# Constant rows, permuted weights and bias copies move from POOL and VectorE to ScalarE

## The chip, the core and the metric

The kernel runs on one core of a Trainium2 chip. The core has five engines that run side by side, each in the order of its own instruction list: TensorE (PE, matrix products into PSUM), VectorE (DVE), ScalarE (ACT), GpSimd (POOL), and SyncE (SP), whose queue issues the DMA transfers. They meet through semaphores. The metric is the device time in microseconds. Three runs of the kernel before gave 901.6, 899.2 and 897.36 us, median 899.2.

## The reference

32 sequences of 256 positions x 256 features go through two blocks, each conditioned on a vector of 512 per sequence. Cut to what is computed:

```python
# layer 0, 8 heads of 32: linear attention
xn = ln(x, ln_w, ln_b)
q = softmax(xn @ Wq + bq, over the 32 features of a head)
k = softmax(xn @ Wk + bk + (1 - mask) * -1e6, over the positions)
v = (xn @ Wv + bv) * mask
y = q @ (k.T @ v)                      # per head
scale, shift = split(silu(emb) @ W_emb + b_emb)
x = x + silu(ln(y) * (1 + scale) + shift) @ W_out + b_out
# layer 1, 16 heads of 16: full attention, other weights
att = softmax(q @ k.T + (1 - mask) * -1e6)   # 256 x 256 per head
y = att @ v
x = x + silu(ln(y) * (1 + scale) + shift) @ out_w + out_b
```

## The kernel before

The work is cut into pieces, each a small function of a sequence number `b` (some also of a part `u`): `s0` (statistics of x), `r0`, `z0` (normalise), `k0`, `q0`, `v0` (projections of layer 0), `km`, `ke` (maximum and exponential of k), `att`, `y0`, `th0`, `st0`, `o0`, `x1` (its output), then `z1`, `q1p`, `k1p`, `v1p`, `rows`, `max`, `cols`, `exp`, `pv`, `yt`, `ty`, `Y1`, `th1`, `o1`, `o` for layer 1. At the bottom of each engine's block stands a written-out list of calls, such as `nmz(); cst(); fill(); r0(0); r0(1); z0(0)`, and this list alone sets the engine's order. Many sequences are in flight at a time. The PSUM bank of each piece comes from the table `BANK`, and the piece that must have freed it from `FREED`.

Projections are products of fp16 parts: a weight is scaled, its high part is written by ScalarE (`high_part`, pieces `wh_q0` to `wh_v1`), its low part by VectorE (`low_part`, pieces `wl_...`, which wait for `wh_...`). Before that come the scales: `w_max` (`w0m`, `w1m`), transposes on TensorE (`tr_...`), `largest` (`mx_...`), a spread over partitions (`ar_...`), `w_scale` (`w0p`, `w1p`). The products of a normalisation bias with weights are rows (`row0` to `row3`, line 928), summed with the bias (`bias_sum`, `fr0` to `fr2`), spread over the partitions (`bb0` to `bb2`, line 935) and copied to SBUF (`bias_copy`, `bc0` to `bc2`). `p3` splits the bias of k in three, and SP carries it to `augs`. The two conditioning tables are `fm0` and `fm1` (line 971), made into factors by `film_rows` (`f0m`, `f1m`) and `film_scale`.

Three parts of the set-up matter here. `fill` (line 2020, on POOL) writes the constant 2^15 into 32 of each 64 partitions of `SQ` and `SK`, the fp16 operands of layer 1's attention; the transfers into them wait for it (`split_in`). `perm` (line 1523, on VectorE) copies the q and k weights of layer 1 with their columns in another order into `XB1`, for the product `col`. `bias_copy` (line 1357, on VectorE) is a copy of 128x256 out of PSUM. A piece of the set-up tells the others that it is done by the counter `C` of its engine, at the place that the table `SETUP` gives it; `ready` waits for that.

Of the kernel before, what the change touches and what calls it, by code (L numbers as in the profile page):

```python
# [17 lines left out]
H1 = 16  # L18

HALF = 64  # L20
# [18 lines left out]
    "gv1": "72527115761226524122121136246323",
    "gr0": "46620260422044626446044242024444",  # L40
    "gr1": "24044600264202262024620426246462",
    "gr2": "46400264226044666646462262644020",
    "gr3": "62604662246226666004464226020044",
    "gr4": "40446460420640004662042444066602",
    "gr5": "62624420620024602666002626044024",
    "gr6": "46444206026246624464626644660662",
    "gr7": "60202466666446202466404426046406",
    "gc0": "06262420644400260046262442044666",
    "gc1": "62602042460624226464644666606040",
# [11 lines left out]
    "gty1": "13103676330420003004000052224650",
    "gy1T": "17523022013501451212002510120455",
    "go1": "62131214011661340161313412022400",
    "gpm": "0",
    "grow3": "2",
    "gcnd": "5",
    "gcol": "6",
    "grow0": "0",
    "gbb0": "3",
    "grow1": "1",  # L70
    "gbb1": "4",
# [2032 lines left out]
```

## Time and profile before

| what | value |
|---|---|
| median of three runs | 899.2 us |
| the profiled execution | 900.0 us |
| its span, from first to last instruction | 898.2 us |
| TensorE busy / mean granted clock | 830.1 us (92%) / 0.969 |
| VectorE busy | 810.9 us (90%) |
| POOL busy | 749.4 us (83%) |
| ScalarE busy | 685.3 us (76%) |
| DMA, mean | 96 GB/s |

The span is that of one profiled execution; a busy share is a mean over stages with different limits, so the windows say more than this table. In a timeline row a merged row "x4" gives the time of four instructions together, and the bracket the idle time before it and what ended it. The granted clock is a share of TensorE's full 2.4 GHz; 0.50 is 1.2 GHz.

### The profile page before, as it was taken

How to read it: one execution, taken by the hardware profiler on the slowest of the kernel's cores; microseconds unless marked ns; L12 is line 12 of the kernel's file. 1: busy time of each engine (PE TensorE's matmuls, PEld its weight loads, DVE VectorE, ACT ScalarE, POOL GpSimd, SP SyncE). 2: the span in 40 equal slices, each digit the busy share in tenths (PEclk: the TensorE clock that was granted, in tenths of full speed). 3: DMA queues.
4: the chain of work that ended last, by engine and by line, in shares of the span. 5: the costliest groups of instructions: out<-in, count | busy, mean ns of one | idle time of the engine just before them, and what ended most of it. 6: DMA issues, size and time to landing. Idle time of an engine off the chain costs nothing.

```text
span 898.2 us, 25197 instructions
## 1 busy us (share of the span) xinstructions
PE 830.1 (92%) x8651; PEld 600.1 (67%) x8651; DVE 810.9 (90%) x1646; ACT 685.3 (76%) x1236; POOL 749.4 (83%) x1210
## 2 busy tenths in 40 slices
PE   4798789899999999999999999999999999999885
PEld 1686766567767767777767777766777776655442
DVE  6999998999999999999999999989999999887862
ACT  0135448598889788889889889887888888888695
POOL 9957799888889889998999899988999887876314
PEclk8598899999999999999999999999999999999998
DMA  7220334433345454352443443464433432334301
GB/s 228 57 42 23 88 73 108 115 96 96 91 87 112 102 111 121 82 119 78 112 112 96 118 111 79 100 111 113 113 86 97 106 89 72 106 81 124 103 30 36
DMA packets 149306, 85.84 MB, mean 96 GB/s; under 512 B 87478, under 2 KB 141852, under 8 KB 149180
## 3 DMA queue, kind: packets, MB, share of 16 engines
q1 hardware_dynamic: 149180, 84.23, 38.1%
q8 instruction: 71, 1.16, 0.5%
q14 instruction: 55, 0.45, 0.2%
HBM read 39.52 MB, written 25.79 MB: 73 GB/s over the span
## 4 chain that ended last, share of the span: by engine, by line
PE 44%; DVE 26%; POOL 15%; issue 10%; ACT 3%; DMA 1%; SPq 1%; POOLq 0%; DVEq 0%; ACTq 0%
PE banks L686 13%; DVE NM L1245 9%; PE banks L833 6%; PE banks L694 5%; PE banks L820 4%; PE banks L809 4%; PE banks L701 3%; DVE st L1146 3%; PE banks L716 2%; PE banks L843 2%; POOL Z L1900 2%; POOL ZHL L1907 2%; PE banks L763 2%; PE banks L752 2%; POOL YN L1891 2%
## 5 line engine op out<-in xcount | busy, mean ns | idle before, releaser
L1245 DVE TENSOR_REDUCE NM<-banks 128x4 f32<-128x1024 f32 x256 | 302.1, 1210 | 14.6 <-PE banks L809 13.9
L1737 ACT ACTIVATE wraw<-banks,uu 128x1024 f32<-128x1024 f32 x154 | 170.8, 1134 | 24.7 <-PE banks L820 23.1
L1737 ACT ACTIVATE PX<-banks,uu 128x1024 f32<-128x1024 f32 x102 | 112.7, 1136 | 14.4 <-PE banks L820 12.7
L1945 POOL TENSOR_TENSOR SH<-ST,SH 128x512 f16<-128x512 f32 x64 | 74.4, 1168 | 33.1 <-ACT SH L1705 33.0
L686 PE MATMUL banks<-wo,SH 128*128 128x256 f16 x768 | 96.2, 277 | 5.2 <-POOL SH L1945 5.1
L1887 POOL TENSOR_TENSOR rs<-ve,nhalf 128x2 f32<-128x2 f32 x128 | 91.9, 718 | 10.7
L809 PE MATMUL banks<-SK,SQ 51*128 51x256 f16 x1024 | 89.8, 272 | 10.4 <-DVE NM L1245 4.0
L820 PE MATMUL banks<-SQ,SK 53*128 53x256 f16 x1024 | 90.5, 273 | 6.2 <-DVE NM L1245 2.2
L686 PE MATMUL banks<-wv,ZT 128*128 128x256 f16 x768 | 94.3, 273 | 2.1 <-DVE NM L1245 1.7
L1907 POOL TENSOR_TENSOR ZHL<-Z,ZHL 128x256 f16<-128x256 f32 x128 | 85.4, 688 | 5.3
L833 PE MATMUL banks<-wraw,V 128*32 128x256 f32 x1232 | 87.1, 385 | 2.6 <-DVE V L1187 1.4
L1719 ACT ACTIVATE R<-banks,fcs,sqs 128x256 f32<-128x256 f32 x128 | 73.2, 572 | 19.2 <-PE banks L694 18.9
L686 PEld LDWEIGHTS banks<-wo,SH 128*128 128x128 f16 x768 | 73.2, 99 | 21.6 <-POOL SH L1945 7.1
L686 PEld LDWEIGHTS banks<-wv,ZT 128*128 128x128 f16 x768 | 72.8, 98 | 17.3 <-issue 9.2
L1973 POOL TENSOR_TENSOR AB<-R,AB 128x512 f16<-128x512 f32 x64 | 76.0, 1193 | 5.2 <-ACT AB L1719 5.1
L1900 POOL TENSOR_SCALAR Z<-X,nm,rs 128x256 f32<-128x256 f32 x128 | 75.7, 599 | 3.2 <-issue 0.2
L1692 ACT ACTIVATE TH<-banks,hB,hA 128x256 f32<-128x256 f32 x128 | 66.4, 581 | 15.3 <-PE banks L701 15.2
L1891 POOL TENSOR_SCALAR YN<-Y,nm,rs 128x256 f32<-128x256 f32 x128 | 71.8, 569 | 2.6
L809 PEld LDWEIGHTS banks<-SK,SQ 51*128 51x128 f16 x1024 | 37.8, 94 | 53.8 <-issue 27.5
L1719 ACT ACTIVATE AB<-banks,fcs,sqs 128x256 f16<-128x256 f32 x128 | 73.6, 575 | 0.0
L820 PEld LDWEIGHTS banks<-SQ,SK 53*128 53x128 f16 x1024 | 37.1, 94 | 47.6 <-issue 26.4
L1663 ACT ACTIVATE KE<-banks,km,un 128x256 f32<-128x256 f32 x64 | 36.3, 585 | 40.4 <-DVE km L1161 37.8
(181 smaller groups left out, 1987.2 us busy)
## 6 DMA issues: line engine op xcount, KB each, us to landing
scr<-AB SPq DMA_DIRECT2D x64, 256.0 KB, 2.7
X<-in_x_dram SPq DMA_DIRECT2D x32, 256.0 KB, 2.9
SQ<-scr SPq DMA_DIRECT2D x64, 128.0 KB, 2.7
SK<-scr SPq DMA_DIRECT2D x64, 128.0 KB, 2.9
out_dram<-wemb SPq DMA_DIRECT2D x32, 256.0 KB, 2.5
SQ<-scr SPq DMA_DIRECT2D x64, 64.0 KB, 2.7
SK<-scr SPq DMA_DIRECT2D x64, 64.0 KB, 2.9
wemb<-in_L_cond_W_emb_dram SPq DMA_DIRECT2D x1, 1024.0 KB, 7.5
```

The costliest lines, as they stand in the source:

```text
L686: m = PE.matmul(dst[:, t, :], zt[:, j, k, t * P:(t + 1) * P], w[:, i, k, :], start=(k, n) == (0, 0), stop=(k, n) == (1, 2))
L809: m = PE.matmul(banks[:, n + j % 2, (j // 2) * T:(j // 2) * T + T], SQ[p, r, h, c * P:(c + 1) * P], SK[p, r, h, :], start=True, stop=True)
L820: m = PE.matmul(banks[:, n + j % 2, (j // 2) * T:(j // 2) * T + T], SK[p, r, h, c * P:(c + 1) * P], SQ[p, r, h, :], start=True, stop=True)
L833: m = PE.matmul(banks[32 * j:32 * j + 32, n, 0:T], V1[:, r, c, 4 * g + j, :], px((8 * b + u) % 5)[:, at_px(j):at_px(j) + T], start=(c == 0 ...
L1245: V.tensor_reduce(NMe[:, c, :, 2 * g:2 * g + 2], banks[:, n:n + 2, :].rearrange("p a (h m) -> p a h m", m=T), AX.X, ALU.max, negate=True). ...
L1719: t = A.activation(dst, bank(home(f"g{c}1", b))[:, f, :], ACT.Identity, bias=fcs[:, i, f:f + 1], scale=sqs[:, i:i + 1])
L1737: A.activation(px(v % 5), banks[:, n:n + 2, :].rearrange("p a n -> p (a n)"), ACT.Exp, scale=uu[:, 0:1]).then_inc(S["exp"])
L1887: G.tensor_tensor(rs[:, b % 2, l, :], ve[:, l, :], nhalf[:, :], ALU.pow).then_inc(S[f"r{l}"])
L1891: i = G.tensor_scalar(dst[:, t, :], src[:, t, :], nm[:, b % 2, l, t:t + 1], rs[:, b % 2, l, t:t + 1], ALU.add, ALU.mult)
L1900: i = G.tensor_scalar(Z[:, t, :], src[:, t, :], nm[:, b % 2, 2 * l, t:t + 1], rs[:, b % 2, 2 * l, t:t + 1], ALU.add, ALU.mult)
L1907: i = G.tensor_tensor(h[:, 1, k], z[:, :, k, :], h[:, 0, k], ALU.subtract)
L1973: G.tensor_tensor(AB[:, i, :, 1], R1[:, i], AB[:, i, :, 0], ALU.subtract).then_inc(S["sp" + c])
```

## The change

`fill` leaves POOL and becomes four pieces of ScalarE, `fill_q0`, `fill_q1`, `fill_k0`, `fill_k1`, each one instruction of 32 partitions x 6144 elements that reads a column of ones with the scale 2^15. `perm` and `bias_copy` go from VectorE to ScalarE word for word, as activations of the kind Identity. The transfers into `SQ` wait for the two fills of `SQ`, those into `SK` for the two of `SK`. The memset of `NMw` (`nmz`) goes behind those of the constants. All lists of calls and the tables `BANK` and `FREED` are written anew for this.

```diff
 SETUP = {
     "DVE": (
-        "mb0 mc w0m csl mx_w0 fr0 fr1 perm w0p w1m csT p3 bc0 wl_q0 bc1 o1m o0m wl_k0 fr2 wl_v0 f0m bm mx_w1 "
...
+        "mb0 csl csT w1m fr2 fr1 w0m mx_w1 fr0 mc mx_w0 w1p w0p o1m wl_q1 p3 wl_v0 wl_k0 o0m f1m f0m wl_q0 "
...
     "ACT": (
-        "th wh_k0 wh_v0 wh_q0 wh_o0 wh_k1 wh_q1 wh_v1 wh_o1 ").split(),
+        "th fill_k1 fill_q0 fill_k0 wh_q1 wh_k1 wh_q0 bc0 wh_v0 wh_k0 perm wh_v1 bc1 fill_q1 wh_o0 bc2 wh_o1 ").split(),
     "POOL": (
-        "nmz cst fill v1z ").split(),
+        "cst v1z nmz ").split(),
...
-        spare = sb("spare", [P, 2])
...
-                    ready(e, "fill")
+                    ready(e, f"fill_{c}0", f"fill_{c}1")
...
 @block.vector
-            def bias_copy(i):
-                ready(e, f"bb{i}")
-                V.tensor_copy(bbc[:, i, :], at_all(i)).then_inc(C["DVE"])
...
-            def perm():
-                e.wait_ge(l_row, 96)
-                e.wait_ge(l_w[1], 80)
-                for i in range(2):
-                    V.tensor_copy(prow[:, i, :].rearrange("p (e f h) -> p e f h", e=2, f=16),
-                                  brow1[:, i, :].rearrange("p (h e f) -> p e f h", e=2, f=16))
-                    for k, e0 in ((0, 0), (0, 1), (1, 0), (1, 1)):
-                        t = V.tensor_copy(XB1[:, i, k, e0 * P:(e0 + 1) * P].rearrange("p (f h) -> p f h", f=16),
-                                          wraw[:, 3 + i, k, :].rearrange("p (h e f) -> p e f h", e=2, f=16)[:, e0])
-                t.then_inc(C["DVE"])
...
 @block.scalar
+            def perm():
+                e.wait_ge(l_row, 96)
+                e.wait_ge(l_w[1], 80)
+                for i in range(2):
+                    A.activation(prow[:, i, :].rearrange("p (e f h) -> p e f h", e=2, f=16),
+                                 brow1[:, i, :].rearrange("p (h e f) -> p e f h", e=2, f=16), ACT.Identity)
+                    for k, e0 in ((0, 0), (0, 1), (1, 0), (1, 1)):
+                        t = A.activation(XB1[:, i, k, e0 * P:(e0 + 1) * P].rearrange("p (f h) -> p f h", f=16),
+                                         wraw[:, 3 + i, k, :].rearrange("p (h e f) -> p e f h", e=2, f=16)[:, e0], ACT.Identity)
+                t.then_inc(C["ACT"])
+
+            def bias_copy(i):
+                ready(e, f"bb{i}")
+                A.activation(bbc[:, i, :], at_all(i), ACT.Identity).then_inc(C["ACT"])
...
+            def fill(M, h):
+
+                ready(e, "cst")
+                r = slice(HALF * h + 32, HALF * h + 64)
+                A.activation(M[r].rearrange("p r h t -> p (r h t)"), one1[r, :].to_broadcast([32, 3 * H1 // 2 * T]), ACT.Identity,
+                             scale=2.0 ** 15).then_inc(C["ACT"])
+
+            def fill_q0():
+                fill(SQ, 0)
+
...
 @block.gpsimd
-            def fill():
-
-                follow(G.memset(spare[:, :], 0.0))
-                for M in (SQ, SK):
-                    for h in range(2):
-                        i = G.memset(M[HALF * h + 32:HALF * h + 64, :, :, :], 2.0 ** 15)
-                        if M is SQ or h == 0:
-                            follow(i)
-                i.then_inc(C["POOL"])
-                ready(e, "fill")
...
```

On ScalarE, the start of the program was (`th` writes SQ, then the high parts of the weights, then the first exponential):

```order
L1772 ACTIVATE SQ<-SQ 32x512
L1762 ACTIVATE wk<-wraw,sl 128x256 x2
L1762 ACTIVATE wv<-wraw,sl 128x256 x2
L1762 ACTIVATE wq<-wraw,sl 128x256 x2
L1663 ACTIVATE KE,ks<-banks,km,un 128x256 x2
L1672 ACTIVATE KT<-banks,mcol 128x256 x2
L1663 ACTIVATE KE,ks<-banks,km,un 128x256 x2
L1679 ACTIVATE QE<-QS 128x512
```

Now ScalarE begins with

```order
L1792 ACTIVATE SQ<-SQ 32x512
L1775 ACTIVATE SK<-one 32x6144
L1775 ACTIVATE SQ<-one 32x6144
L1775 ACTIVATE SK<-one 32x6144
L1739 ACTIVATE wq<-wraw,sl 128x128 x4
L1739 ACTIVATE wk<-wraw,sl 128x128 x4
L1739 ACTIVATE wq<-wraw,sl 128x256 x2
```

and behind the pieces of `perm` and one more weight its list reads, up to the first exponential,

```order
L1754 ACTIVATE XB<-wraw 128x128 x4
L1739 ACTIVATE wv<-wraw,sl 128x256 x2
L1760 ACTIVATE bbc<-banks 128x256
L1775 ACTIVATE SQ<-one 32x6144
L1640 ACTIVATE KE,ks<-banks,km,un 128x256 x2
L1649 ACTIVATE KT<-banks,mcol 128x256 x2
```

Three fills stand ahead of the first weight, and the high parts of both layers, bias copies, `perm` and the fourth fill all ahead of the first `KE`.

On POOL, behind the constants, the first normalisation (`nm`, `ve`, `rs`, then `Z`) was

```order
L2015 MEMSET augm 6x768
L2022 MEMSET spare 128x2
L2025 MEMSET SQ 32x6144 x2
L2025 MEMSET SK 32x6144 x2
L1885 TENSOR_SCALAR nm<-mv 128x2
L1886 TENSOR_SCALAR ve<-mv 128x2
L1887 TENSOR_TENSOR rs<-ve,nhalf 128x2
```

Now POOL goes, from the last constant to the memset of V,

```order
L2036 MEMSET augm 6x768
L1906 TENSOR_SCALAR nm<-mv 128x2
L1907 TENSOR_SCALAR ve<-mv 128x2
L1908 TENSOR_TENSOR rs<-ve,nhalf 128x2
L1906 TENSOR_SCALAR nm<-mv 128x2
L1907 TENSOR_SCALAR ve<-mv 128x2
L1908 TENSOR_TENSOR rs<-ve,nhalf 128x2
L1921 TENSOR_SCALAR Z<-X,nm,rs 128x256 x2
L1925 TENSOR_SCALAR ZHL<-Z 128x256 x2
L1928 TENSOR_TENSOR ZHL<-Z,ZHL 128x256 x2
L2042 MEMSET V 128x3072
L2043 MEMSET V 128x96
```

The memsets of `SQ` and `SK` are gone; that of `V`, which stood behind five normalisations, comes right behind the first.

On TensorE, ahead of the first large products (`wq` or `wk` with `ZT`), where line 971 (973 now) is a conditioning table and line 988 the product `col`, stood

```order
L989 MATMUL banks<-one,SQ 128x1
L988 MATMUL banks<-lnc,XB 128x1 x2
L989 MATMUL banks<-one,SQ 128x1
L988 MATMUL banks<-lnc,XB 128x1 x2
L989 MATMUL banks<-one,SQ 128x1
L971 MATMUL banks<-csT,wemb 128x32 x16
L863 MATMUL banks<-ident,mxw 3x128
L686 MATMUL banks<-wq,ZT 128x256 x12
L716 MATMUL banks<-ZT,wk 128x256 x6
L718 MATMUL banks<-augm,augs 128x256
L716 MATMUL banks<-ZT,wk 128x256 x6
```

Now TensorE has, between the last spread maxima and the first projections,

```order
L871 MATMUL banks<-mxd,ones 128x3
L937 MATMUL banks<-SQ,ones 128x256
L871 MATMUL banks<-mxd,ones 128x3
L973 MATMUL banks<-csT,wemb 128x32 x32
L718 MATMUL banks<-ZT,wk 128x256 x6
L720 MATMUL banks<-augm,augs 128x256
L718 MATMUL banks<-ZT,wk 128x256 x6
L720 MATMUL banks<-augm,augs 128x256
L688 MATMUL banks<-wv,ZT 128x256 x12
L865 MATMUL banks<-ident,mxw 1x128
L990 MATMUL banks<-lnc,XB 128x1 x2
L991 MATMUL banks<-one,SQ 128x1
```

Both conditioning tables are made ahead of the first projection, `col` is behind it, and k0 comes before q0.

On SP, the loads of layer 1's weights (`ld_w1`) now go out ahead of those of layer 0, with the load of the third sequence between them, and the six bias rows (`ld_r`) behind both.

## Rows read from the trace of the kernel before

**Rows 1.** The page, section 1: busy us, share of the span, instructions.
```profile
PE 830.1 (92%) x8651; PEld 600.1 (67%) x8651; DVE 810.9 (90%) x1646; ACT 685.3 (76%) x1236; POOL 749.4 (83%) x1210
```
**Rows 2.** Windows of the span: length, busy us by engine, granted clock, DMA.
```profile
0.00:41.20 41.20, 22.70 (x87) 17.04 (x88) 33.84 (x69) 4.41 (x8) 38.33 (x46) 0.70 0.53 145
32.00:39.00 7.00, 6.92 (x32) 6.90 (x32) 6.76 (x18) 0.23 (x1) 6.49 (x12) 0.50 0.21 39
41.20:160.00 118.80, 104.07 (x848) 84.95 (x848) 109.24 (x302) 63.28 (x139) 97.96 (x161) 0.89 0.31 72
160.00:800.00 640.00, 625.22 (x6830) 455.99 (x6832) 603.72 (x1165) 541.71 (x972) 567.14 (x934) 1.00 0.41 100
```
**Rows 3.** Timeline of POOL: start, duration, engine, line, operation, out<-in, idle before.
```profile
5.81 10.48 POOL L2025 MEMSET SQ<- 32x6144 f16 x2
16.35 11.97 POOL L2025 MEMSET SK<- 32x6144 f16 x2
28.41 0.19 POOL L1885 TENSOR_SCALAR nm<-mv 128x2 f32<-128x2 f32 x1
...
69.18 2.67 POOL L2032 MEMSET V<- 128x3072 f32 x1
```
**Rows 4.** Timeline of VectorE, the start and three later points.
```profile
14.57 1.75 DVE L1287 TENSOR_SCALAR mxd<-ident,mxc 3x3 f32<-3x3 f32 x1
...
17.07 5.39 DVE L1527 COPY SQ<-SK 1x256 f32<-1x256 f32 x1
22.39 0.77 DVE L1530 COPY XB<-wraw 128x128 f32<-128x128 f32 x4
...
23.26 5.09 DVE L1309 TENSOR_SCALAR pw<-sw 128x3 int32<-128x3 int32 x1
...
58.64 0.30 DVE L1309 TENSOR_SCALAR pw<-sw 128x3 int32<-128x3 int32 x1
...
79.33 0.75 DVE L1225 SCALAR_TENSOR_TENSOR X<-banks,un,XB 128x512 f32<-128x512 f32 x1
...
122.40 4.61 DVE L1245 TENSOR_REDUCE NM<-banks 128x4 f32<-128x1024 f32 x4
```
**Rows 5.** The page, section 5: ScalarE's largest group, count, busy, mean ns.
```profile
L1737 ACT ACTIVATE wraw<-banks,uu 128x1024 f32<-128x1024 f32 x154 | 170.8, 1134 | 24.7 <-PE banks L820 23.1
```
**Rows 6.** Timeline of ScalarE, three short pieces.
```profile
48.23 0.56 ACT L1663 ACTIVATE KE<-banks,km,un 128x256 f32<-128x256 f32 x1 [16.00 <-DVE km L1161]
...
54.86 0.62 ACT L1679 ACTIVATE QE<-QS 128x512 f32<-128x512 f32 x1
...
60.54 1.76 ACT L1762 ACTIVATE wk<-wraw,sl 128x128 f16<-128x128 f32 x4 [0.95 <-DVE iu L1330]
```
**Rows 7.** Timeline of SP's queue: two issues among the first loads.
```profile
7.74 0.47 SPq L495 DMA_DIRECT2D lnc<-in_L_cond_norm_b_dram  x1
...
16.32 1.53 SPq L499 DMA_DIRECT2D wemb<-in_L_cond_emb_w_dram  x1
```
**Rows 8.** DMA issues of the first 60 us: KB each, us to landing.
```profile
wemb<-in_L_cond_emb_w_dram SPq DMA_DIRECT2D x1, 1024.0 KB, 7.8
...
lnc<-in_L_cond_norm_b_dram SPq DMA_DIRECT2D x1, 1.0 KB, 4.4
```
**Rows 9.** Timeline of TensorE in the first 100 us.
```profile
9.71 4.31 PE L928 MATMUL banks<-wraw,lnc 128*1 128x256 f32 x12 [3.39 <-DMA lnc<-in_L_cond_ln_b_dram]
...
32.08 7.04 PE L971 MATMUL banks<-csT,wemb 128*128 128x32 f32 x32 [2.99 <-DVE csT L1490]
...
63.15 3.66 PE L971 MATMUL banks<-csT,wemb 128*128 128x32 f32 x32
...
90.76 1.12 PE L701 MATMUL banks<-ident,QE 128*128 128x128 f32 x4 [3.89 <-ACT QE L1679]
...
94.95 1.47 PE L694 MATMUL banks<-ZT,wq 128*128 128x256 f16 x12
```

More of the change, by code:

```diff
@@ L39 @@
[L39 to L49, printed above, removed]
@@ L61 @@
[L61 to L71, printed above, removed]
+    "gk0": "00614615174301150224341111057220",
+    "gkt": "67450610124020220001013203004504",
+    "gq0": "47140221473664301312012232346031",
+    "gqt": "14667341121140174315313330371050",
+    "gv0": "33116143505014241003200420210402",
@@ L88 @@
+    "ga_f0": "1",
+    "gt_f1": "7",
+    "ga_f1": "3",
+    "gt_b": "3",
+    "ga_b": "4",
     "gfm0": "1",
@@ L255 @@
     "PE": (
-        "pm row1 row0 row3 tr_w0 row2 ar_w0 bb0 bb1 cnd col fm0 tr_w1 tr_b tr_o0 tr_f0 ar_o0 ar_w1 ar_f0 "
-        "tr_o1 ar_o1 fm1 ar_b tr_f1 ar_f1 bb2 ").split(),
+        "cnd pm row2 row1 tr_w1 row0 row3 bb2 tr_w0 bb1 ar_w1 bb0 ar_w0 fm1 fm0 tr_o0 col tr_f0 ar_o0 ar_f0 "
+        "tr_o1 tr_f1 ar_o1 tr_b ar_b ar_f1 ").split(),
     "DVE": (
-        "mb0 mc w0m csl mx_w0 fr0 fr1 perm w0p w1m csT p3 bc0 wl_q0 bc1 o1m o0m wl_k0 fr2 wl_v0 f0m bm mx_w1 "
-        "mx_f0 mx_o0 o0p mx_o1 w1p film0 mx_b wl_k1 f1m wl_o0 mx_f1 fcs o1p wl_q1 mb1 wl_v1 bc2 film1 wl_o1 ").split(),
+        "mb0 csl csT w1m fr2 fr1 w0m mx_w1 fr0 mc mx_w0 w1p w0p o1m wl_q1 p3 wl_v0 wl_k0 o0m f1m f0m wl_q0 "
+        "wl_k1 mx_o0 wl_v1 mx_f0 o0p film0 mx_o1 wl_o0 bm mx_b o1p mx_f1 fcs mb1 film1 wl_o1 ").split(),
     "ACT": (
-        "th wh_k0 wh_v0 wh_q0 wh_o0 wh_k1 wh_q1 wh_v1 wh_o1 ").split(),
+        "th fill_k1 fill_q0 fill_k0 wh_q1 wh_k1 wh_q0 bc0 wh_v0 wh_k0 perm wh_v1 bc1 fill_q1 wh_o0 bc2 wh_o1 ").split(),
     "POOL": (
-        "nmz cst fill v1z ").split(),
+        "cst v1z nmz ").split(),
 }
@@ L1473, in fr2 @@
                 bias_sum(2)
-            def bc0():
-                bias_copy(0)
-            def bc1():
-                bias_copy(1)
-            def bc2():
-                bias_copy(2)
             def csl_():
@@ L1562, in fcs_ @@
                 V.tensor_scalar(tm[:, :], tm[:, :], 2.0 ** -15, None, ALU.mult).then_inc(C["DVE"])
-            mb0(); s0(0); s0(1); mc(); w0m(); csl_(); mx_w0(); fr0(); fr1(); perm(); w0p(); w1m(); csT_(); p3_()
-            bc0(); wl_q0(); s0(2); bc1(); o1m(); o0m(); wl_k0(); fr2(); wl_v0(); f0m(); bm(); q1(0); km(0)
-            mx_w1(); qm(0); v(0); s0(3); mx_f0(); s0(4); rk(0); mx_o0(); km(1); at_(0); v(1); q1(1); o0p(); rq(0)
-            qm(1); mx_o1(); w1p(); Y0(0); q1(2); rk(1); film0(); mx_b(); qm(2); s1(0); v(2); at_(1); km(2); rq(1)
@@ L1653, in _ @@
-            o_(31)
+            mb0(); csl_(); s0(0); s0(1); csT_(); s0(2); w1m(); fr2(); fr1(); w0m(); mx_w1(); fr0(); mc(); mx_w0()
+            w1p(); w0p(); o1m(); wl_q1(); p3_(); wl_v0(); wl_k0(); o0m(); f1m(); s0(3); f0m(); wl_q0(); s0(4)
+            wl_k1(); mx_o0(); km(0); wl_v1(); v(0); mx_f0(); rk(0); q1(0); o0p(); qm(0); v(1); film0(); q1(1)
+            mx_o1(); km(1); qm(1); at_(0); rq(0); km(2); q1(2); Y0(0); qm(2); s1(0); rk(1); rq(1); at_(1); wl_o0()
+            q1(3); Y0(1); v(2); qm(3); s1(1); st0(0); rq(2); rk(2); q1(4); at_(2); qm(4); bm(); km(3); x1(0)
@@ L1768, in high_out, with bc0, bc1, bc2 @@
                 A.activation(W["o", l][:, 0], worw[:, l], ACT.Identity, scale=sw[:, 6 + l:7 + l]).then_inc(C["ACT"])
+            def perm():
[11 more added lines that the diff above has]
+                A.activation(bbc[:, i, :], at_all(i), ACT.Identity).then_inc(C["ACT"])
+            def bc0():
+                bias_copy(0)
+            def bc1():
+                bias_copy(1)
+            def bc2():
+                bias_copy(2)
+            def fill(M, h):
[5 more added lines that the diff above has]
+                fill(SQ, 0)
+            def fill_q1():
+                fill(SQ, 1)
+            def fill_k0():
+                fill(SK, 0)
+            def fill_k1():
+                fill(SK, 1)
             def th():
@@ L1796, in wh_o1 @@
                 high_out(1)
-            th(); wh_k0(); wh_v0(); wh_q0(); ke(0); kt(0); ke(1); qe(0); qt(0); wh_o0(); kt(1); qe(1); wh_k1()
-            qt(1); qe(2); th0(0); ke(2); sh0(0); kt(2); ke(3); wh_q1(); wh_v1(); qt(2); kt(3); ke(4); th0(1)
-            sh0(1); qe(3); qa(0); qt(3); ka(0); qe(4); kt(4); th0(2); qt(4); ke(5); sh0(2); kt(5); qe(5); wh_o1()
-            qt(5); th0(3); sh0(3); qa(1); ka(1); ke(6); kt(6); qa(2); qe(6); th0(4); ka(2); sh0(4); qt(6); ke(7)
-            th0(5); kt(7); exp(0, 0); exp(0, 1); exp(0, 2); exp(0, 3); exp(0, 4); exp(0, 5); sh0(5); qe(7)
@@ L1868, in _ @@
-            yt(31, 1); yt(31, 2); yt(31, 3); sh1(29); th1(30); sh1(30); th1(31); sh1(31)
+            th(); fill_k1(); fill_q0(); fill_k0(); wh_q1(); wh_k1(); wh_q0(); bc0(); wh_v0(); wh_k0(); perm()
+            wh_v1(); bc1(); fill_q1(); ke(0); kt(0); qe(0); wh_o0(); qt(0); ke(1); bc2(); qe(1); qt(1); kt(1)
+            qe(2); ke(2); th0(0); kt(2); sh0(0); qe(3); qt(2); ke(3); th0(1); ke(4); sh0(1); qe(4); qt(3); kt(3)
+            kt(4); qa(0); th0(2); sh0(2); ka(0); ke(5); qa(1); ka(1); wh_o1(); kt(5); qt(4); qe(5); th0(3); sh0(3)
```

832 lines of the change are left out of this document (423 added, 409 removed), and 215 rows, old and new, of the table FREED.

## The prediction

> **What bounds the kernel now.** I read the page first. TensorE is busy for 92% of the span and VectorE for 90% [rows 1], so either could be the bound, and only stretches tell. In the windows of the span [rows 2] the reader is to see three kernels in one. From 160 to 800 us TensorE is busy for 625.2 of 640 us at full clock: it sets the pace there, and nothing off it matters. In the first 41.2 us it is busy for 22.7 us only, at a mean clock of 0.70, and between 41.2 and 160 it idles for 118.8 - 104.07 = 14.7 us and runs at a mean clock of 0.89. The change touches instructions of the start alone, so its worth is how much earlier TensorE is fed. A start that comes earlier passes through the full stretch one for one.
>
> Next I read POOL's timeline [rows 3]. Four memsets (helper `fill`, 32 rows x 6144 fp16 each, in two merged rows) take it from 5.81 to 28.32 us, and only then does it normalise the first sequence (28.41). Then VectorE's timeline in the same stretch [rows 4]. Instructions of a few elements last as long as a memset does: the cast of 3 columns at 23.26 takes 5.09 us and ends at 28.35, with POOL's memsets; the same form takes 0.30 us at 58.64. The copy of one row of 256 at 17.07 takes 5.39 us and ends at 22.46, again with a memset. The product with `ident` at 14.57 takes 1.75 us and ends at 16.32. Four copies of 128x128 at 22.39 are not held (0.77 together). So VectorE loses about 1.5 + 5.1 + 4.8 = 11.4 us behind fills. The trace shows this; it is the mechanism on which the forecast rests.
>
> The Trainium skill, "SBUF — State Buffer" (the section on engine ports), says that VectorE and GpSimd share one port pair as an exclusive lock, that the loser waits for the whole instruction, and that ScalarE never waits on anyone. By that rule the stall vanishes wholly when ScalarE writes the same bytes, and it stays for whatever POOL memset is left. The trace agrees for the copies and casts named, while the 128x128 copies show that not every VectorE instruction pays.
>
> **The change part by part.** (1) Removed from POOL: `fill`, 22.5 us. POOL is then free at about 5.3 us; it gets `z0(0)` to `z0(4)` done long before the weights need them. Alone this is worth nothing: after 28.41 [rows 3] z0(0) still came before its weights. What is late next is the weights' path.
>
> (2) Removed from VectorE: the waits of 11.4 us; `perm`, which without waits is 2 x 0.77 for the eight copies and about 2 x 0.2 for the rows, 1.9 us; three copies of a bias, 3 x 0.4 = 1.2 us. Together 14.5 us. Left on POOL is the memset of `V1`, 2.67 us [rows 3], now right behind `z0(0)`, at about 12 us. There VectorE is in a long reduction or waits for DMA, so I charge 0 and keep 2.7 us as the upper bound.
>
> (3) Added on ScalarE: four fills of 6144 elements a row. No such long instruction is in the trace. From 512 elements (0.62 us [rows 6]) to 1024 (1.134 us [rows 5]) an element costs 1.0 ns, so a fill is 0.62 + 5632 x 0.001 = 6.2 us. Bounds: the same slope from zero, 6.1 us; and the price per element of the 128-wide pieces of `wk`, 1.76 us for 4 x 128, 3.4 ns [rows 6], 21 us, which is far. I take 6.2, since a fill is one long instruction, nearest to the 1024 row. Three fills stand before the weights: from the end of `cst` (5.5 us) to 24.1. Then wh_q1 1.7, wh_k1 1.7, wh_q0 0.8, bc0 0.4, wh_v0 0.8, wh_k0 0.8: 30.3 us. Then `perm`, ten pieces of 0.35 to 0.45, 3.6; wh_v1 0.8, bc1 0.4, the fourth fill: 41.3 us. Queued behind it is `ke(0)`, for which the whole first chain waits.
>
> (4) Moved on SP: the weights of layer 1 come first, those of layer 0 five weight issues and one X issue later. In before the first set of weights releases TensorE at 9.71 [rows 9]; the second set's last vector is issued at 7.74 and lands 4.4 us later [rows 7, 8]. So layer 1 is now there at 9.7 and layer 0 at 7.74 + 0.51 + 4.4 = 12.7. The six bias rows go out last at 10.9; with the same 4.4 us they are there at 15.3. The last tables of the second embedding land, as now, near 24 (the 1 MB issue at 16.32 takes 7.8 [rows 7, 8]).
>
> Walk of the start, in the new order, each step at the sum of its own rows in the timelines of before. TensorE: rows of layer 1 from 9.7, those of layer 0 from 12.7, at 0.36 to 0.47 us a matmul of which a row has four (12 took 4.31 [rows 9]); with the broadcasts, 1.0 each, and the transposes, ar_w1 ends at 21.4 and ar_w0 at 23. VectorE: biases from 15.3, w0m and the maxima until 20.3, w1p (1.9) 23.3, w0p 25, o1m 25.7, wl_q1 27.6, p3 (4.1 now) 31.7, wl_v0 and wl_k0 by 33.4. TensorE meanwhile makes both embedding tables. One took 7.04 us at half clock, 3.66 at full [rows 9]. In before the first ran for 7 us at 0.50 throughout [rows 2], so I charge both 7.04: 23 to 37.1 us. So `k0(0)`, the first large matmul, starts at 37.1, 4.1 us before q0(0) at 41.2, with the second table done (3.66 us at 63.15 no longer to do): TensorE is 4.1 + 3.7 = 7.8 us ahead there.
>
> VectorE goes on: o0m, f1m, s0(3) to 37.5, f0m 40, wl_q0, s0(4), wl_k1 43.9, mx_o0, `km(0)` 45.2, wl_v1, `v(0)` 46.8. In before km(0) releases ke(0) at 48.23 [rows 6], and v(0) ends at 49.9: 3 us ahead. But by then it has also done w1p, wl_q1, f1m, wl_k1, wl_v1, mx_o0 and s0(3), 1.9 + 1.9 + 2.6 + 1.9 + 0.9 + 0.4 + 1.0 = 10.6 us that before does later, and has left out q1, qm and bm, 1.8. It is thus 3 + 10.6 - 1.8 = 11.8 us ahead in work. `ke(0)` waits for km(0) at 45.2 and not for the fourth fill at 41.3: the fill is hidden by 3.9 us. Following the new order with these durations, `x1(0)` comes at about 72 to 73 against 79.33 [rows 4], `q1p(0)` near 84 against 94.95 [rows 9], and the first maximum of `rows(0)` at 111 to 113 against 122.40 [rows 4]. Being 10 us early there, TensorE must lose less in the ramp: in before its clock fell to half after waits such as the 3.89 us in front of 90.76 [rows 9], for ScalarE's QE, itself late by VectorE's rq.
>
> Sum against the profiled execution, 900.0 us (span 898.2 plus 1.8 around it): 7.8 us at the start, 2 to 4 more of the 14.7 idle us of the ramp, nothing in the full stretch, nothing in the tail: -10.5, thus 889.5. The median of the three runs is 0.8 lower, so 889. For the new order in the long stretch and the tail, which the trace of before cannot show, I allow 3 us either way.
>
> **The rivals.** (A) As above, 889, own range 885 to 893. (B) Given back: TensorE starts 4 us early, but the ramp keeps its waits since the transposes, copies and scratch transfers that feed layer 1 are as long as before; then only the start counts, 900 - 4 = 896 to 899. For it: POOL is busy for 97.96 of the ramp's 118.8 us [rows 2] and can bound it whatever VectorE does. Against it: part of that load is backlog of the fill. (C) More: all 14.5 us of VectorE arrive at the end, since it is busy for 109.2 of 118.8 us in the ramp [rows 2], or the tables run at full clock, which brings k0(0) to where its `augs` rows land, about 35, and runs the first matmuls at twice the speed, 2 + 3 us. That gives 900 - 14.5 = 885.5, or with both some 882. The Trainium skill, "TensorE: Matmul & The Clock Gate" (Part 1), says that a TensorE kept busy is given the full clock. By that rule the tables would be this faster case; the 7 us at 0.50 in the trace speak against it. (D) Slower: the price of a fill. If a 6144-element row on ScalarE costs like short pieces, with the 256-wide step of 0.45 us (1.76 ns an element) it is 10.8 us. Then the weights leave ScalarE at 44.1 instead of 30.3, and the fourth fill ends at 5.5 + 4 x 10.8 + 11.0 of the rest = 59.7, with ke(0) behind it, against 48.23 in before [rows 6]. That is 11.5 us late, less the 3.7 of the table: 908. It decides from about 8.8 us a fill, where ke(0) would be 3.7 us late. (E) It doesn't do what it says, VectorE being held by other POOL work that moves into the gap: as B.
>
> **How the numbers follow.** A 0.58, B with E 0.13, C 0.23, D 0.06. The range 881 to 897 leaves out D, the upper edge of B and the far end of C, under 2 in 10. What this kernel's measurement can tell from no change is 0.5%, 4.5 us. Below 894.7 lie A, C: 0.82. Within are most of B and a sliver of A: 0.12. Slower: D, 0.06.
>
> **What would show it.** Right: ScalarE's fills at 6 to 6.5 us each; no VectorE instruction of a few elements over 1 us before 40 us; first k0(0) matmul at 35 to 38; q1p(0) near 84; TensorE's busy time from 160 to 800 about as now. Wrong: fills over 8 us, ke(0) released by a fill, k0(0) after 41, or the ramp with as much idle as before although VectorE is ahead.

## The result, and the profile after

The changed kernel takes 878.1 us (median of 4 runs, 877.98 to 878.67); the kernel before took 898.4 beside it (897.36 to 901.6). The ratio is 0.9761, 95% interval 0.9730 to 0.9792: 2.4% faster. Forecast were 889 and a range of 881 to 897. The sign was right; the gain of 20.3 us by the medians (21.5 by the ratio) is twice the predicted 10, and the time lies outside the range. One of the eight runs of `new_fillback` below took 1599 us and is left out of its figures.

The profiled execution of after took 878.06 us, its span 876.2, so 22.0 less than the span of before. Section 1 of its page, against [rows 1]:

```profile
PE 827.4 (94%) x8651; PEld 603.3 (69%) x8651; DVE 792.1 (90%) x1633; ACT 708.0 (81%) x1253; POOL 725.7 (83%) x1205
```

TensorE does the same work in nearly the same busy time (830.1 and 827.4), so 19.3 of the 22.0 us are idle time of TensorE and 2.7 are busy time. POOL has 23.7 us less to do, VectorE 18.8 less, ScalarE 22.7 more. ScalarE's timeline shows the new fills, against none in [rows 6]:

```profile
5.27 5.32 ACT L1775 ACTIVATE SK<-one 32x6144 f16<-32x6144 f32 x1 [1.08 <-POOL augm L2036]
10.62 5.32 ACT L1775 ACTIVATE SQ<-one 32x6144 f16<-32x6144 f32 x1
15.85 5.30 ACT L1775 ACTIVATE SK<-one 32x6144 f16<-32x6144 f32 x1
22.34 1.72 ACT L1739 ACTIVATE wq<-wraw,sl 128x128 f16<-128x128 f32 x4 [1.19 <-DVE iu L1332]
...
32.99 5.32 ACT L1775 ACTIVATE SQ<-one 32x6144 f16<-32x6144 f32 x1
43.18 0.56 ACT L1640 ACTIVATE KE<-banks,km,un 128x256 f32<-128x256 f32 x1 [4.88 <-DVE km L1163]
```

A fill takes 5.32 us (6.2 predicted). The first weight waits 1.19 us for VectorE's scale and `ke(0)` 4.88 us for VectorE's maximum: neither waits for a fill. VectorE's timeline, against [rows 4]:

```profile
19.70 0.17 DVE L1311 TENSOR_SCALAR pw<-sw 128x3 int32<-128x3 int32 x1
19.90 0.64 DVE L1312 TENSOR_SCALAR pw<-pw 128x3 f32<-128x3 f32 x1
20.57 0.59 DVE L1314 TENSOR_SCALAR pw<-pw 128x2 f32<-128x2 f32 x1
...
26.08 1.12 DVE L1444 TENSOR_SCALAR augs<-augs,iu 6x256 bf16<-6x256 bf16 x1
27.12 1.36 DVE L1445 TENSOR_SCALAR SQ<-SQ,iu 1x256 f32<-1x256 f32 x1
```

The cast that took 5.09 us behind a memset takes 0.17. What is left of such waits is 0.4 to 1.1 us each, behind POOL's ordinary tensor operations:

```profile
19.84 1.29 POOL L1928 TENSOR_TENSOR ZHL<-Z,ZHL 128x256 f16<-128x256 f32 x2
25.85 2.50 POOL L1947 TENSOR_TENSOR XB<-X,bobc 128x512 f32<-128x512 f32 x2 [4.71 <-DMA bobc<-in_L_cond_b_out_dram]
```

TensorE's timeline of the start, against [rows 9]:

```profile
9.65 1.86 PE L930 MATMUL banks<-wraw,lnc 128*1 128x256 f32 x4 [1.79 <-DMA lnc<-in_L_cond_norm_b_dram]
13.00 1.87 PE L930 MATMUL banks<-wraw,lnc 128*1 128x256 f32 x4 [1.49 <-DMA lnc<-in_L_cond_ln_b_dram]
...
20.05 13.59 PE L973 MATMUL banks<-csT,wemb 128*128 128x32 f32 x64
33.49 1.44 PE L718 MATMUL banks<-ZT,wk 128*128 128x256 f16 x6
```

The weights come at 9.7 and 13.0 (9.7 and 12.7 predicted) and both tables take 13.6 us (14.1 predicted). But they start at 20.05, not at 23, and `k0(0)` at 33.5, not 37.1.

**Where the 22 us are.** I cut both spans at the same work: at the first large product, at the output of sequence 0 (`o(0)`), of sequence 14 and of 25, the points read off VectorE's timeline. Before:

```profile
41.20:206.30 165.10, 147.02 (x1307) 115.21 (x1308) 153.88 (x383) 97.17 (x201) 136.58 (x227) 0.92 0.34 81
...
206.30:553.00 346.70, 342.79 (x3755) 253.27 (x3754) 329.28 (x648) 298.04 (x537) 315.92 (x521) 1.00 0.43 103
553.00:812.40 259.40, 250.45 (x2744) 178.34 (x2740) 241.99 (x461) 219.23 (x389) 224.42 (x366) 1.00 0.39 97
812.40:898.20 85.80, 67.11 (x770) 36.20 (x768) 51.95 (x91) 66.45 (x104) 34.13 (x54) 0.97 0.24 68
```

After:

```profile
33.50:191.80 158.30, 144.38 (x1295) 112.00 (x1296) 143.23 (x357) 99.44 (x197) 133.15 (x224) 0.93 0.36 83
...
191.80:538.30 346.50, 340.81 (x3739) 253.85 (x3739) 329.37 (x644) 293.92 (x532) 314.68 (x519) 1.00 0.41 101
538.30:792.00 253.70, 250.11 (x2764) 181.42 (x2764) 240.56 (x467) 220.24 (x389) 223.98 (x367) 1.00 0.43 104
792.00:876.20 84.20, 68.63 (x768) 38.52 (x756) 52.14 (x91) 65.51 (x103) 35.22 (x55) 0.90 0.22 63
```

The first number behind each window is its length. The lengths differ by 6.8, 0.2, 5.7 and 1.6 us, and the start before them by 7.7: together 22.0. So 14.5 us are gained up to 192 us (`o(0)`); the next 347 us of work take the same time; then, long after all that the change replaced is done, another 7.3 come. In the third window TensorE idles for 8.95 us before (259.40 - 250.45) and 3.6 after. Which part comes from the placement of the work (who does it) and which from the new order and banks is what the experiments have to tell.

### The profile page after: what moved, and what is told of

It reads as the page before. It is cut to its first block, busy times and chain, and to the rows that moved or that the text cites. A ratio compares the mean times of both kernels' runs of the same rounds, so it can differ in the third digit from the quotient of the medians.

```text
span 876.2 us, 25220 instructions
## 1 busy us (share of the span) xinstructions
PE 827.4 (94%) x8651; PEld 603.3 (69%) x8651; DVE 792.1 (90%) x1633; ACT 708.0 (81%) x1253; POOL 725.7 (83%) x1205
## 4 chain that ended last, share of the span: by engine, by line
PE 39%; POOL 19%; DVE 14%; issue 11%; ACT 5%; DMA 0%; SPq 0%; POOLq 0%; DVEq 0%; ACTq 0%
PE banks L688 11%; PE banks L835 7%; DVE NM L1247 4%; PE banks L696 4%; PE banks L822 4%; PE banks L811 4%; POOL ZHL L1928 3%; PE banks L703 3%; POOL Z L1921 3%; DVE st L1148 2%; PE banks L845 2%; POOL YN L1912 2%; POOL SH L1966 2%; POOL ZHL L1925 2%; POOL AB L1994 2%
## 5 line engine op out<-in xcount | busy, mean ns | idle before, releaser
L1714 ACT ACTIVATE PX<-banks,uu 128x1024 f32<-128x1024 f32 x102 | 112.9, 1138 | 11.4 <-PE banks L822 9.9
L688 PE MATMUL banks<-wv,ZT 128*128 128x256 f16 x768 | 98.6, 280 | 0.9 <-DVE NM L1247 0.8
L1696 ACT ACTIVATE R<-banks,fcs,sqs 128x256 f32<-128x256 f32 x128 | 73.5, 574 | 26.7 <-PE banks L696 20.3
L1928 POOL TENSOR_TENSOR ZHL<-Z,ZHL 128x256 f16<-128x256 f32 x128 | 87.8, 706 | 5.3
L688 PEld LDWEIGHTS banks<-wv,ZT 128*128 128x128 f16 x768 | 74.8, 100 | 17.3 <-issue 7.5
L835 PE MATMUL banks<-wraw,V 128*32 128x256 f32 x1232 | 85.1, 385 | 1.6 <-ACT wraw L1714 0.6
L1669 ACT ACTIVATE TH<-banks,hB,hA 128x256 f32<-128x256 f32 x128 | 66.2, 580 | 15.7 <-PE banks L703 14.2
L1906 POOL TENSOR_SCALAR nm<-mv 128x2 f32<-128x2 f32 x128 | 29.0, 226 | 49.0 <-DVE mv L1151 48.2
```

Source lines behind the costliest of these rows:

```text
L688: m = PE.matmul(dst[:, t, :], zt[:, j, k, t * P:(t + 1) * P], w[:, i, k, :], start=(k, n) == (0, 0), stop=(k, n) == (1, 2))
L835: m = PE.matmul(banks[32 * j:32 * j + 32, n, 0:T], V1[:, r, c, 4 * g + j, :], px((8 * b + u) % 5)[:, at_px(j):at_px(j) + T], start=(c == 0 ...
L1696: t = A.activation(dst, bank(home(f"g{c}1", b))[:, f, :], ACT.Identity, bias=fcs[:, i, f:f + 1], scale=sqs[:, i:i + 1])
L1714: A.activation(px(v % 5), banks[:, n:n + 2, :].rearrange("p a n -> p (a n)"), ACT.Exp, scale=uu[:, 0:1]).then_inc(S["exp"])
L1928: i = G.tensor_tensor(h[:, 1, k], z[:, :, k, :], h[:, 0, k], ALU.subtract)
```

## The experiments

Before ran in each group on the same chip: median 901.1, 900.5 and 900.9. "Lead" below is how much earlier a kernel starts the output of a sequence than before does, in one profiled execution of each (`x1` is the output of layer 0, `o` that of layer 1):

```
lead (us) at    x1(0)  o(0)  o(10)  o(14)  o(20)  o(25)  span
after            9.1   14.5   13.5   14.7   17.9   20.3   22.0
old_fill        10.0   10.0   10.1   10.1   11.5   10.5   10.9
old_all         12.9   14.2   14.4   14.4   16.0   16.0   12.3
new_fillback   -10.0   -4.2   -5.5   -4.3   -1.4    1.0    2.7
new_allback    -10.1   -8.1   -9.0   -7.8   -5.3   -2.4    0.2
late_new         0.1    0.6    0.5   -1.2    0.9    3.8    5.4
late_old        10.1   11.5   10.3   10.1   10.8   10.9    9.9
tail_new         0.2    0.2    0.1    0.2    1.7   -2.3    1.5
fill_behind     -8.8   -8.7   -8.4   -8.3   -6.8   -6.7   -7.5
pool_late        5.4    7.0    6.9    6.9    8.2    8.2    4.4
fill_more        2.4    4.4    1.9    3.1    5.9    8.2   11.0
```

### Four corners: placement and order apart

`old_fill` keeps the lists and banks of before; only the four fills move to ScalarE. `old_all` moves `perm` and the bias copies too. Their ScalarE lists:

```diff
-th(); wh_k0(); wh_v0(); wh_q0(); ke(0); kt(0); ke(1)
+th(); fill_k1(); fill_q0(); wh_k0(); wh_v0(); wh_q0(); fill_k0(); fill_q1(); ke(0); kt(0); ke(1)    # old_fill
+th(); fill_k1(); perm(); wh_k0(); wh_v0(); wh_q0(); bc0(); bc1(); fill_q0(); fill_k0(); ke(0)       # old_all, fill_q1 behind wh_k1
```

> Order, banks and everything else of before; only the four fills are moved from POOL to ScalarE (two behind th, two behind wh_q0). Placement theory (the gain is VectorE and POOL freed from behind the memsets): k0(0) starts 5 us or more earlier than at 44.1, no VectorE instruction of a few elements above 1 us before 30 us, and the time is 885 to 890. Order theory (the gain lies in the order found anew, which uses the freed engines): the first large matmul comes earlier, but the old lists give it back in waits, 893 to 899.

> As old_fill, and perm and the three bias copies on ScalarE too, in the order of before. Placement theory: 2 to 3 us below old_fill, 883 to 888, since VectorE has 3.1 us less to do on the path. Order theory: the same as old_fill within 1.5 us.

Measured: old_fill 889.2 us, ratio 0.9876 (0.9854 to 0.9898); old_all 887.5, 0.9865 (0.9840 to 0.9889). old_fill lies in the range of the placement theory and outside that of the order theory. VectorE's timeline of old_fill at the place of [rows 4]:

```profile
18.47 0.46 DVE L1206 TENSOR_SCALAR pw<-sw 128x3 int32<-128x3 int32 x1
...
37.34 0.69 DVE L1057 TENSOR_REDUCE km<-banks 128x2 f32<-128x512 f32 x1 [0.69 <-PE banks L615]
```

The cast stands 4.8 us earlier (18.47 against 23.26) and ends 9.4 earlier; the first maximum of k, at 47.25 in before, comes 9.9 earlier, and the lead from there to 550 us is 10.0 to 10.1. What VectorE gains in the first 40 us is handed through undiminished. In old_all the lead is 14.2 to 14.4 in the same stretch, close to the 14.5 us that the prediction had found for VectorE's relief; its tail then loses 3.7 of it (16.0 to 12.3), which is why perm and copies show only 0.1% in the time. The time of old_all alone decides nothing (1.0 to 1.7 us below old_fill); its lead, 4.2 us more at `o(0)`, does.

The other two corners keep the order and banks of after and put the work back, on POOL in front of its first normalisation and on VectorE.

```diff
-cst(); r0(0); r0(1); z0(0); v1z()            # POOL, after
+cst(); fill(); r0(0); r0(1); z0(0); v1z()    # new_fillback, new_allback (there perm and bias copies go back to VectorE too)
```

> Order and banks of the changed kernel; only the four fills go back to POOL, behind cst. Placement theory: the waits behind memsets come back, 889 to 894. Order theory: 880 to 885, as the new lists put other work there.

> Order and banks of the changed kernel, with fills on POOL and perm and bias copies on VectorE, so the placement of before with the order of after. Placement theory: 892 to 898, nearly all of the gain gone. Order theory: 881 to 887, most of the gain kept. If both hold in parts, the four corners (before, old_all, new_allback, after) give each its share and their interaction.

Measured: new_fillback 897.2 us, 0.9957 (0.9939 to 0.9975); new_allback 899.5, 0.9972 (0.9952 to 0.9992). Both lie above every range named, on the far side of the placement theory; that the order alone keeps the gain is refuted. So of before's time, placement alone takes 1.35%, order alone 0.28%, both 2.39%: some 12, 2.5 and 21.5 us. The rest of about 7 us does not mean that order and placement need each other all along. new_allback is 8.1 us behind at `o(0)` and ends level: its order loses 8 us at the start, where VectorE is held, and gains as much later.

### The later order by itself

`late_new` runs before up to some 555 us (placement of before too) and the order and banks of after from there. `late_old` is the reverse. `tail_new` is before up to 800 us.

```diff
-all lists and BANK of one kernel
+its lists and BANK up to a product of TensorE at 555 (545) us, those of the other behind it    # late_new (late_old)
+the same at 800 us                                                                             # tail_new
```

> The kernel before up to its 756th piece on TensorE (about 555 us: the start of sequence 20's o0) with the other engines as far as they can be by then, and from there on the order and banks of the changed kernel. Placement is that of before throughout. Theory 1, the new order of the second half is worth 7 us by itself: 889 to 893 where before gives 898. Theory 2, the gain past 600 us comes from the earlier start and needs it: 896 to 900.

> The changed kernel up to about 545 us (sequence 20's o0), and from there on the order and banks of before. Theory 1, the order: 883 to 887, with 14.7 us of gain left. Theory 2, the start: 877 to 880. The seam itself may cost up to 2 us in either kernel; it cancels in the sum of late_new and late_old, which theory 1 puts at before plus after.

> The kernel before up to sequence 30's o0 (about 800 us), and the order of the changed kernel for the last 100 us only. If the late gain of 7 us lies in the last stretch alone: 891 to 893. If, as the lag of the outputs says, 5 of it arise between 600 and 800 us: 895 to 897.

Measured: late_new 894.0 us, 0.9923 (0.9907 to 0.9938); late_old 887.8, 0.9858 (0.9837 to 0.9880); tail_new 898.5, 0.9976 (0.9964 to 0.9989). The order behind 550 us gives 0.77% on its own start (6.9 us) and taking it from after costs 0.97% (8.7 us). About 2 us of it lie in the last stretch (0.24%). late_new fits the theory that the order alone does it (6.5 us below its own before, 5 to 9 expected), late_old lies 0.8 us above its range for that theory and far from the other (877 to 880), tail_new 1.5 us above the nearer of its two. The ratios of late_new and late_old add up to those of before and after within 0.2%, so the seams cost little. The profiles say the same more sharply. From `o(14)` to the end of the span the five kernels that have the new order there (after, new_fillback, new_allback, fill_more, late_new) take 337.2 to 338.6 us, whatever their start, and the seven that have the old one up to 800 us (before among them) 343.9 to 347.7. The window of late_new, against 259.40 in before and 253.70 in after:

```profile
552.40:808.30 255.90, 252.13 (x2765) 182.22 (x2767) 239.20 (x459) 219.76 (x389) 222.69 (x364) 0.99 0.39 101
```

TensorE idles for 3.8 us there, as in after (3.6), not 8.95. TensorE's waits in this stretch, summed by what it waited for (total, times, longest), are short ones. Before:

```profile
PE banks L833 <- DVE V L1187: 1.4, 2, 1.1
PE banks L820 <- DMA SQ<-ntd: 1.2, 1, 1.2
PE banks L833 <- DVE Y L1264: 1.1, 2, 0.7
```

After, the three longest:

```profile
PE banks L822 <- ACT wemb L1722: 0.7, 1, 0.7
PE banks L811 <- DVE V1t L1239: 0.5, 1, 0.5
PE banks L845 <- ACT wemb L1722: 0.5, 1, 0.5
```

No single wait carries it, and no run separates the lists from the banks. Which moved piece or bank does it stays open.

### Is it VectorE that is held, or POOL that is late?

`fill_behind` is before with POOL's fill behind its second normalisation, so POOL normalises early and the memsets fall on VectorE's scales and biases.

```diff
-nmz(); cst(); fill(); r0(0); r0(1); z0(0); z0(1); xb0(0)
+nmz(); cst(); r0(0); r0(1); z0(0); z0(1); fill(); xb0(0)
```

> The kernel before with one piece moved: POOL normalises the first two sequences and fills SQ and SK only then (from 16 us on instead of from 5.8). Theory A, the fill costs because VectorE is held behind its memsets: no gain, the held instructions are others, 896 to 903. Theory B, it costs because POOL itself is late for the first sequences: 10 us less, 887 to 891, as with old_fill.

Measured: 909.0 us, 1.0093 (1.0076 to 1.0110), slower than before: theory B is refuted, and theory A's range of 896 to 903 missed on the far side. VectorE's timeline, with POOL's memsets from 18.26 to 40.1:

```profile
19.23 5.08 DVE L1207 TENSOR_SCALAR pw<-sw 128x3 int32<-128x3 int32 x1
24.34 5.24 DVE L1208 TENSOR_SCALAR pw<-pw 128x3 f32<-128x3 f32 x1
29.61 0.18 DVE L1211 RECIPROCAL sw<-pw 128x3 f32<-128x3 f32 x1
29.82 5.02 DVE L1212 TENSOR_SCALAR sw<-sw 128x3 f32<-128x3 f32 x1
```

Each of the three held ones waits out a memset, and a fourth (34.88, 5.23 us) waits out the last. Such an instruction takes 0.17 us without a memset, so that is some 19.9 us of waits against the 11.4 of before, 8.5 more, and the kernel is 8.8 us behind before at x1(0) and 8.3 at o(14): the stall costs what it holds. POOL's early normalisation bought nothing here.

`pool_late` is old_fill with a wait in POOL for the third fill, so that POOL starts nearly as late as in before (26.99 against 28.41 us) while VectorE is free.

```diff
-nmz(); cst(); r0(0); r0(1); z0(0)                       # POOL, old_fill
+nmz(); cst(); ready(e, "fill_k0"); r0(0); r0(1); z0(0)
```

> old_fill (the order and banks of before, the four fills on ScalarE) with one wait more: POOL, free from 5.3 us, waits for the third fill before its first normalisation r0(0), so it starts at about 28.2 us, where before has it at 28.41. POOL gains nothing here; VectorE is still free of POOL's memsets. Theory 1 (the start is worth what VectorE is no longer held): as old_fill, 889 to 891, x1(0) about 10 us ahead of before. Rival 2 (the start is worth that POOL normalises earlier and its backlog is gone): as before, 898 to 901. Between the two, each has a share: z0(0) at 29 to 30 us lies close to the first large product at 31.7 in old_fill, so a share of up to 2 us for POOL would not surprise me.

Measured: 895.9 us, 0.9944 (0.9926 to 0.9962), between the two theories; up to 2 us for POOL had been allowed, and it is 6. TensorE's and VectorE's timelines:

```profile
37.33 2.74 PE L583 MATMUL banks<-wq,ZT 128*128 128x256 f16 x12 [4.70 <-DMA ZT<-ZHL]
```
```profile
28.33 0.75 DVE L1043 BATCH_NORM_STATS2 st<-X 128x6 f32<-128x256 f32 x2 [3.28 <-issue]
...
40.17 0.75 DVE L1068 SCALAR_TENSOR_TENSOR Q<-banks,un,bbc 128x512 f32<-128x512 f32 x1 [3.85 <-PE banks L583]
```

The first product now waits 4.70 us for the normalised sequence 0, and VectorE 3.85 us for that product. VectorE's 3.28 us before have no releaser in the profile; they end as POOL's late first pieces do. The lead at o(0) is 7.0 instead of 10.0. So freeing VectorE is the gain, and POOL's earlier start is what lets 3 of its 10 us arrive. (1) of the prediction, that POOL's relief is worth nothing alone, agrees with fill_behind; beside VectorE's relief it is worth 3 us of lead, and 0.68% (6 us) of the time, since this kernel loses another 3.8 us of its lead in the tail (8.2 to 4.4).

### How much slack the fills have

`fill_more` is after with an extra activation of 32 x 4096 ahead of each of the three front fills: 10.7 us more for ScalarE, as if a fill cost 8.9 us.

```diff
             def fill(M, h):
+                if M is SK or h == 0:
+                    A.activation(PX2[w]..., one1[w, :].to_broadcast([32, 16 * T]), ACT.Identity, scale=2.0 ** 15)
                 A.activation(M[r]..., one1[r, :].to_broadcast([32, 3 * H1 // 2 * T]), ACT.Identity, scale=2.0 ** 15)
```

> The kernel after, with one more activation of 32 x 4096 (about 3.6 us) in front of each of the three fills that stand ahead of the weights: ScalarE has 10.7 us more to do before the first weight, as if such a fill cost 8.9 us. In after ScalarE waits 1.19 us for VectorE ahead of the first weight and 4.88 us for km(0) ahead of ke(0). Theory 1 (what the start loses passes on one for one): the high parts are 9.5 us later, VectorE's low parts stand behind them in its list, k0(0) comes at 39 to 41 instead of 33.5, ke(0) at 48 to 50 instead of 43.2, x1(0) 5 to 7 us later, and the time is 883 to 886. Rival 2 (the prediction's break point: from 8.8 us a fill nothing of the gain is left at the start): 888 to 892, since only the gain of the later order stays. Rival 3 (the start has slack, TensorE makes it up in the ramp): 878 to 881.

Measured: 887.9 us, 0.9837 (0.9812 to 0.9862), so 6.8 us (by the ratios) to 9.8 (by the medians) over after, and 11.0 in the span. TensorE's, VectorE's and ScalarE's timelines:

```profile
41.01 1.44 PE L718 MATMUL banks<-ZT,wk 128*128 128x256 f16 x6 [7.07 <-DMA augs<-p]
```
```profile
33.66 1.45 DVE L1345 SCALAR_TENSOR_TENSOR wq<-wraw,sl,wq 128x128 f16<-128x128 f32 x4 [8.82 <-ACT wq L1739]
```
```profile
31.82 1.73 ACT L1739 ACTIVATE wq<-wraw,sl 128x128 f16<-128x128 f32 x4
...
50.70 0.56 ACT L1640 ACTIVATE KE<-banks,km,un 128x256 f32<-128x256 f32 x1 [2.93 <-DVE km L1163]
```

The first product is 7.5 us late, at 41.0 (39 to 41 expected), and `ke(0)` 7.5 us late, at 50.7 (48 to 50); VectorE's low part of `wq` is 9.4 us late (33.66 against 24.29 in after), and the lead at o(0) falls by 10.1. x1(0) is 6.7 us later (5 to 7 expected). Theory 1 has the mechanism; its time (883 to 886) and that of rival 2 (888 to 892) both touch the interval, which is 884 to 888.5 us, so the time alone does not part them. The loss follows VectorE's delay, not TensorE's. Rival 3 is refuted. At o(0), 4.4 us of the start are still left, so 8.9 us for each of the three front fills is not yet the break point that the prediction saw at 8.8. The fourth fill kept its 5.3 us here. `ke(0)` waited 2.93 us for `km(0)`, so 3.6 us more in that fill would have moved it by some 0.7 us (an estimate).

## Why the prediction was wrong, point by point

**Right.** TensorE's full stretch passes a lead on one for one: 10.0 to 10.1 in old_fill from x1(0) to o(14). The mechanism, VectorE held behind memsets. Both tables at half clock (13.59 us against 14.1). Landings at 9.7 and 13.0. x1(0) at 70.25 (72 to 73 predicted) came a little earlier than the walk had it, the first maximum of rows(0) at 111.65 (111 to 113) where it had it. The fills hidden: `ke(0)` released by `km(0)`. Rival D's price did not come (5.32 us a fill), and fill_more shows that it would have been dear: 10.7 us of ScalarE cost 10.1 of lead.

**The first step that failed: "TensorE is 4.1 + 3.7 = 7.8 us ahead there".** The walk put the tables at 23; they started at 20.05. It let VectorE's weight maxima wait for the bias rows at 15.3, and charged `ar_w0` after them. After has the first bias at 13.91, the maxima from 15.25 and `ar_w0` done at 20.1. With 7.7 for the start and 3.7 for the second table the lead was 11.4, not 7.8.

**The ramp, "2 to 4 more", was right in size.** The window from the first product to o(0) is 6.8 us shorter, 3.7 of it the second table: 3.1. But the reason was not TensorE's waits. The walk had also given VectorE's lead: km(0) 3 us ahead plus 8.8 of later work done. Measured, km(0) starts at 42.22 against 47.25, 5.0 ahead, and 5.0 + 8.8 = 13.8 is close to the 14.5 of o(0). The prediction had this second sum (11.8) beside the first (10.5) and took the one that counts TensorE. VectorE was busy for 109.2 of 118.8 us in the ramp [rows 2]; its lead in work was the one to carry. old_all confirms it with unchanged lists: the 14.5 us of relief named in part (2) arrive as 14.2 to 14.4. That the sum fits so well is partly luck: the fills, charged with 11.4, gave 10.0 (old_fill), and perm and copies, charged with 3.1, gave 4.2 of lead. It was rival C's size, 885.5, with 0.23.

**The second step that failed: "nothing in the full stretch, nothing in the tail", with 3 us either way for the order.** 5.7 us came between o(14) and o(25), 1.6 behind it. late_new and late_old show this to be the new order (with its banks), by 7 to 9 us, independent of what was moved at the start, and tail_new puts some 2 us of it behind 800 us. The sentence "TensorE is busy for 625.2 of 640 us ... nothing off it matters" was true and hid this: 14.8 idle us were left, half of them (7.5) between 553 and 800 us, and new lists for the whole program could take them. A bound of 3 us for rewriting all lists had no row behind it; TensorE's idle time where it is "full" would have been that row: it gives 15 in the stretch and 18.7 in the last window (85.80 - 67.11).

**Sum.** 11.4 + 3.1 + 7.3 = 21.8, with 0.2 between o(0) and o(14) the 22.0 of the spans; predicted were 7.8 + 2.7 + 0. Of the 11.5 us that the forecast missed, 3.6 belong to the first failed step and 7.3 to the second.

**Of the rivals.** B (given back) is refuted by the lead of after, 9.1 us at x1(0) and 14.5 at o(0). C was right for the start in its first half, VectorE's relief; its second, the tables at full clock, did not come (and 885.5 less 2 + 3 is 880.5, not 882). The chances of A and C sum to 0.81, so 0.82 below 894.7 leaves nothing of A for the middle. The Trainium skill, "TensorE: Matmul & The Clock Gate" (Part 1), has a busy TensorE given the full clock; the 13.59 us of the tables disagree. E: POOL work that stays holds VectorE by 0.4 to 1.1 us a time, five times between 13 and 29 us, some 3 us together and not 11.

**A misread row.** The prediction took the four copies of 128x128 at 22.39 [rows 4] as a sign that some instructions pass a memset. They did not pass it. The memset waited for them: each memset of `SK` took 0.75 us longer than those of `SQ`, about the 0.77 us of the four copies that stood beside its start.

```profile
5.81 5.21 POOL L2025 MEMSET SQ<- 32x6144 f16 x1
16.35 5.97 POOL L2025 MEMSET SK<- 32x6144 f16 x1
22.37 5.95 POOL L2025 MEMSET SK<- 32x6144 f16 x1
```

The sum of 11.4 us does not use these copies.

**What would show it.** Fills 5.3 us, just below the 6 to 6.5 named. "No VectorE instruction of a few elements over 1 us" held (0.64); two row operations of 256 took 1.1 and 1.4. TensorE's busy time from 160 to 800, "about as now", is 629.8 against 625.2: a third of its idle time there is gone, and that sign of the late gain was named and expected not to move. k0(0) at 33.5 lay before the 35 to 38, q1p(0) at 86.3 behind the 84:

```profile
86.31 1.47 PE L696 MATMUL banks<-ZT,wq 128*128 128x256 f16 x12
```

That q1p(0) was only 8.6 us ahead while o(0) was 14.5 ahead shows that one early event of a reordered program does not measure its lead: q1p(0) is placed elsewhere in the order.

## What to carry to other kernels

Where two engines are near their limit in a ramp, compute the lead of each in work done, not only the time of the next event, and carry that of the engine which is busier there; with unchanged lists the two were close (first large product and o(0): 9.7 and 10.0 us ahead in old_fill, 11.8 and 14.2 in old_all), with new lists they were not (7.7 and 14.5 in after). When a change rewrites the order of the whole program, bound its effect by the idle time of the bounding engine in every stretch, the full one and the tail too, and not by a small allowance. A long memset on POOL belongs where VectorE runs none of the small scalings and copies that it holds, or on an engine with slack in front of its first due piece.
